# Turning the second batch's normalised input for a linear-attention and FFN kernel: squares of 32 on VectorE and a pass through memory in place of four TensorE transposes

## What is computed

```python
x = x + layernorm(attn(layernorm(x)))
x = x + layernorm(ffn(layernorm(x)))

def attn(h):                                   # 32 heads of 128, blocks of 32 tokens
    q, k, v = silu(h @ qkv_w.T)                # per head
    # scan over blocks with a decayed state kv
    out = (q k^T * diag_decay) v + (q * q_decay) kv
    kv  = kv * block_decay + (k * k_decay)^T v
    return (sigmoid(h @ gate_w.T) * norm_w * rmsnorm(out)) @ out_w.T
def ffn(h):                                    # ternary weights with scales, 512 -> 1792 -> 512
    return (silu(h @ gate.T) * (h @ up.T)) @ down.T
```

## Time and profile before

| what | value |
|---|---|
| median of 3 runs | 2406.01 us (2404.29 to 2406.74) |
| the profiled execution's own time | 2405.24 us |
| its span in the profile | 2403.2 us |
| PE busy | 2355.4 us, 98% of the span, 12276 matmuls |
| DVE busy | 1383.0 us, 58% |
| ACT busy | 1208.9 us, 50% |
| POOL busy | 1679.1 us, 70% |
| DMA | 307.15 MB, mean 128 GB/s |
| granted TensorE clock | 0.995 of full speed over the span |

### The profile page before, as it was taken

How to read it: one execution, slowest core, us unless ns; L and a number is a source line. 1 busy time by engine, 2 the same in 40 slices (tenths; PEclk the granted TensorE clock), 3 DMA queues, 4 the chain that set the end, 5 groups by cost and what they waited for, 6 DMA issues and landing times.

```text
span 2403.2 us, 38344 instructions
## 1 busy us (share of the span) xinstructions
PE 2355.4 (98%) x12276; PEld 2005.5 (83%) x12276; DVE 1383.0 (58%) x2475; ACT 1208.9 (50%) x1748; POOL 1679.1 (70%) x1322
## 2 busy tenths in 40 slices
PE   7999999999999999989999999999999999899997
PEld 6788888888888888878888888888888888788886
DVE  5555555555666666646555555555555555555655
ACT  5555555554444444435454555544444444366563
POOL 4777777777777777756777777777777776474675
PEclk9999999999999999999999999999999999999999
DMA  4344443444444444454444334443333334512212
GB/s 136 127 131 138 137 131 123 134 142 142 145 142 133 129 134 142 156 195 145 141 140 131 126 127 131 131 140 127 119 118 109 109 109 141 181 56 77 79 62 97
DMA packets 165953, 307.15 MB, mean 128 GB/s; under 512 B 22384, under 2 KB 102256, under 8 KB 163184
## 3 DMA queue, kind: packets, MB, share of 16 engines
q1 hardware_dynamic: 138992, 269.93, 34.5%
q10 hardware_dynamic: 26880, 36.18, 4.6%
HBM read 219.02 MB, written 87.03 MB: 127 GB/s over the span
## 4 chain that ended last, share of the span: by engine, by line
PE 86%; ACT 3%; DMA 3%; issue 3%; DVE 3%; POOL 1%; SPq 0%; DVEq 0%; ACTq 0%; POOLq 0%
PE proj L1994 53%; PE yp L1994 18%; PE sc L2041 4%; PE sc L2064 4%; PE sc L2067 4%; PE sc L2054 3%; DMA k_blocks<-pd 1%; DVE pd L1498 1%; ACT piece L1006 0%; ACT k L915 0%; DMA v_tok<-v_blocks 0%; ACT L915 0%; DMA v_blocks<-vf 0%; DMA fs_stage<-ffn_scales 0%; ACT sq L929 0%
## 5 line engine op out<-in xcount | busy, mean ns | idle before, releaser
L1994 PE MATMUL proj<-xb,w_odd 128*128 128x512 f32 x2694 | 705.1, 399 | 5.3 <-ACT g L899 1.8
L1994 PE MATMUL proj<-xb,w_even 128*128 128x512 f32 x2694 | 680.5, 396 | 11.9 <-DMA xb<-x_blocks 3.9
L1994 PEld LDWEIGHTS proj<-xb,w_even 128*128 128x128 f32 x2694 | 498.6, 189 | 114.1 <-issue 7.9
L1994 PEld LDWEIGHTS proj<-xb,w_odd 128*128 128x128 f32 x2694 | 489.5, 189 | 104.6 <-DVE q L1469 5.4
L599 POOL TENSOR_TENSOR qd<-q,table 128x512 f32<-128x512 f32 x128 | 164.0, 1294 | 194.2 <-ACT q L915 194.2
L1543 DVE TENSOR_TENSOR g<-sc,g 128x512 f32<-128x512 f32 x128 | 88.5, 691 | 298.2 <-ACT sq L929 298.2
L590 POOL TENSOR_TENSOR ow_lo<-v_tok,ow_hi 128x1024 fp32r<-128x1024 f32 x32 | 76.7, 2396 | 232.1 <-ACT ow_hi L883 232.1
L1550 DVE TENSOR_TENSOR y<-yp,y 128x512 f32<-128x512 f32 x240 | 164.5, 685 | 120.2 <-PE yp L1994 119.3
L1994 PE MATMUL proj<-x_t,f_hi 128*128 128x512 f32 x896 | 214.2, 392 | 2.7 <-issue 2.7
L1994 PE MATMUL yp<-ow_hi,g_hi 128*128 128x512 f32 x512 | 202.4, 395 | 1.3 <-DVE y L1550 1.3
L1994 PEld LDWEIGHTS proj<-x_t,f_hi 128*128 128x128 f32 x896 | 169.1, 189 | 38.2 <-issue 2.9
(11 more groups left out here) (193 smaller groups left out, 4413.2 us busy)
## 6 DMA issues: line engine op xcount, KB each, us to landing
raw<-w_attn SPq DMA_DIRECT2D x128, 512.0 KB, 3.6
k_blocks<-pd SPq DMA_DIRECT2D x64, 512.0 KB, 3.5
k_tok<-k_blocks SPq DMA_DIRECT2D x256, 128.0 KB, 2.8
v_blocks<-vf SPq DMA_DIRECT2D x64, 512.0 KB, 2.7
v_tok<-v_blocks SPq DMA_DIRECT2D x256, 128.0 KB, 2.8
v_tok<-w_out SPq DMA_DIRECT2D x32, 512.0 KB, 4.5
fraw<-w_ints SPq DMA_DIRECT2D x13, 1024.0 KB, 4.9
piece<-w_ints ACTq DMA_DIRECT2D x21, 512.0 KB, 4.3
```

What stands on the lines that cost most here:

```text
L1994: last = pe.matmul(psum, s, m, start=start and n == 0, stop=n == len(terms) - 1, skip_group_check=more)
```

## The change

TensorE's `turn_piece` and ACT's copy out of PSUM are gone. In their place:

1. DVE (`turn_piece(j, i)`, new) turns the same data in squares of 32 within `piece`, with two instructions of 128 x 256 elements, once ACT has normalised both tiles. It stands behind `keep_s2(w, QQ)` and ahead of `gate(a, 0, 1)`.
2. ACT (`piece_there`, new) issues one DMA of 256 KB that writes them to `p_blocks` in device memory, where `keep_piece` stood.
3. ACT (`piece_back_in`, new) waits for that DMA and issues four DMAs of 64 KB that read them back, so that the squares land in their places on the partitions; it stands behind `activate(w, QQ, OUT22)` and ahead of the two `k_decay(w, 1, ...)`.
4. ACT's `keep_piece` waits for these four and copies from `piece` itself, now behind the two `k_decay(w, 1, ...)`.
5. `mix_piece` moves on DVE from behind `finish_21(w, QQ)` to behind `add_out(a, 2)`, and `piece_high` on ACT from ahead of `activate(w, VV, OUT11)` to behind it.
6. TensorE no longer waits for `piece_normed` and `piece_kept`. Its windows w = 2 to 14 are one loop instead of three; DVE's windows w = 2 to 7 are two loops instead of one.

```diff
--- before.py
+++ after.py
@@ -180,6 +180,7 @@
         piece_in = [sem("piece_in0"), sem("piece_in1")]
         piece_step, piece_sd_ready = sem("piece_step"), sem("piece_sd_ready")
         piece_normed, piece_turned, piece_kept = sem("piece_normed"), sem("piece_turned"), sem("piece_kept")
+        piece_out, piece_back = sem("piece_out"), sem("piece_back")
         piece_mixed, piece_hi_done, piece_lo_done = sem("piece_mixed"), sem("piece_hi_done"), sem("piece_lo_done")
         piece_hi_out, piece_lo_out = sem("piece_hi_out"), sem("piece_lo_out")
         xb_in = [sem(f"xb_in{b}") for b in range(NB)]
@@ -273,6 +274,10 @@
         piece_hi = piece[:, 0:NB * P].bitcast(F32R)
         piece_lo = piece[:, NB * P:2 * NB * P]
         mix = piece_lo.rearrange("p (b n) -> p b n", b=NB)
+
+
+        piece_quads = piece[:, 2 * HID:3 * HID].rearrange("p (b m s t) -> p b m s t", b=QUADS, m=2, s=HALVES)
+        piece_t = piece[:, 0:HID]
         kt = pd[:, 0].rearrange("p h c n -> p (h c n)").rearrange("p (b h c d) -> p b h c d",
                                                                 b=QUADS, h=2, c=CH)
         ow = v_tok[:, :, :, :, :].rearrange("p i h c d -> p (i h c d)").rearrange("p (h n) -> p h n", h=2)
@@ -314,6 +319,7 @@
 
         k_blocks = nc.dram_tensor("k_blocks", (HALVES, QUADS, QUAD, QUADS, 2 * CH * QUAD), F32).ap()
         v_blocks = nc.dram_tensor("v_blocks", (HALVES, QUADS, QUAD, QUADS, 2 * CH * QUAD), F32).ap()
+        p_blocks = nc.dram_tensor("p_blocks", (QUADS, QUAD, QUADS, HID // QUADS), F32).ap()
         x_blocks = nc.dram_tensor("x_blocks", (NB, P, 2, RT, SEG), F32).ap()
         attn_first = nc.dram_tensor("attn_first", (BT, P, HID), F32).ap()
         mid_first = nc.dram_tensor("mid_first", (BT, P, HID), F32).ap()
@@ -1008,12 +1014,25 @@
 
             def keep_piece(j):
 
-                act.wait_ge(piece_turned, j + 1)
-                wait(act, piece_lo_out, 16 * j)
+                act.wait_ge(piece_back, 16 * QUADS * (j + 1))
                 for m in range(2):
-                    act.activation(mix[:, B_21 * m:B_21 * m + T_3 + 1:T_3],
-                                   yp[0][:, 2 * P * m:2 * P * (m + 1)].rearrange("p (s n) -> p s n", s=HALVES),
+                    act.activation(mix[:, B_21 * m:B_21 * m + T_3 + 1:T_3]
+                                   .rearrange("p s (i t) -> p s i t", i=QUADS),
+                                   piece_t.rearrange("p (i m s t) -> p m s i t", i=QUADS, m=2, s=HALVES)[:, m],
                                    ACT.Copy).then_inc(piece_kept, 1)
+
+            def piece_there(j):
+
+                act.wait_ge(piece_turned, 2 * (j + 1))
+                act.dma_start(p_blocks.rearrange("i d b n -> (i d) (b n)"),
+                              piece[:, 2 * HID:3 * HID]).then_inc(piece_out, 16)
+
+            def piece_back_in(j):
+
+                act.wait_ge(piece_out, 16 * (j + 1))
+                for b in range(QUADS):
+                    act.dma_start(piece_t[quad(b)].rearrange("d (i n) -> d i n", i=QUADS),
+                                  p_blocks[:, :, b].rearrange("i d n -> d i n")).then_inc(piece_back, 16)
 
             def piece_high(j):
 
@@ -1074,7 +1093,7 @@
                 square(a, 0, 1)
                 gated_hi(a, 0, 1)
                 if part is not None:
-                    keep_piece(part)
+                    piece_there(part)
                 if checks is not None:
                     look_at_ints(checks + 1)
                 if first_done:
@@ -1086,8 +1105,12 @@
                 activate(w, QQ, OUT22)
                 if finish is not None:
                     store_tile(finish)
+                if part is not None:
+                    piece_back_in(part)
                 k_decay(w, 1, 0)
                 k_decay(w, 1, 1)
+                if part is not None:
+                    keep_piece(part)
                 split_hi_s(w, GG)
                 activate(w, QQ, OUT12)
                 split_hi_a(w, GG)
@@ -1096,9 +1119,9 @@
                 k_decay(w, 0, 0)
                 k_decay(w, 0, 1)
                 square(a, 1, 1)
+                activate(w, VV, OUT11)
                 if part is not None:
                     piece_high(part)
-                activate(w, VV, OUT11)
                 gated_hi(a, 1, 0)
                 gated_hi(a, 1, 1)
                 if part is not None:
@@ -1623,6 +1646,14 @@
                 dve.scalar_tensor_tensor(tile_shift[:, :], tile_meanvar[:, :, 0], -1.0, tile_rstd[:, :],
                                          ALU.mult, ALU.mult).then_inc(piece_step, 1)
 
+            def turn_piece(j, i):
+
+                dve.wait_ge(piece_normed, 2 * (j + 1))
+                for m in range(2):
+                    dve.transpose(piece_quads[:, :, m],
+                                  tiles[:, :, chunk(2 * m + i)].rearrange("p s (b t) -> p b s t", b=QUADS))\
+                        .then_inc(piece_turned, 1)
+
             def mix_piece(j):
 
                 dve.wait_ge(piece_kept, 2 * (j + 1))
@@ -1634,7 +1665,7 @@
                 dve.tensor_tensor(mix[:, T_4], mix[:, B_21], mix[:, T_2], ALU.subtract).then_inc(piece_mixed, 1)
 
             def window(w, first=False, checks=None, rms_of=None, ends_first=False, finish=None, begin=None,
-                       part=None, next_part=False):
+                       part=None, part_half=0, next_part=False):
                 a = w - 1
                 if rms_of is not None:
                     rms(rms_of, yp[0])
@@ -1657,6 +1688,8 @@
                 gate(a, 0, 0)
                 finish_21(w, KK)
                 keep_s2(w, QQ)
+                if part is not None:
+                    turn_piece(part, part_half)
                 gate(a, 0, 1)
                 if finish is not None:
                     tile_lo(finish)
@@ -1675,12 +1708,12 @@
                     dve.wait_ge(attn_out[0], 16)
                 add_out(a, 0, first)
                 finish_21(w, QQ)
-                if part is not None:
-                    mix_piece(part)
                 gate(a, 1, 0)
                 add_out(a, 1, first)
                 keep_s2(w, VV)
                 add_out(a, 2, first)
+                if part is not None:
+                    mix_piece(part)
                 if checks is not None:
                     look_at_block(checks + 1, 1)
                 gate(a, 1, 1)
@@ -1770,9 +1803,11 @@
 
             first_window()
             window(1, first=True, part=0, next_part=True)
-            with dve.Fori(2, 2 * CH) as w:
+            with dve.Fori(2, CH + 1) as w:
                 window(w, part=w - 1, next_part=True)
-            window(2 * CH, part=2 * CH - 1)
+            with dve.Fori(CH + 1, 2 * CH) as w:
+                window(w, part=w - 1, part_half=1, next_part=True)
+            window(2 * CH, part=2 * CH - 1, part_half=1)
             with dve.Fori(2 * CH + 1, PAIRS - 1) as w:
                 window(w, checks=CHECKS_PER_WINDOW * (w - 2 * CH - 1))
             window(PAIRS - 1, checks=WIDTH_CHECKS - CHECKS_PER_WINDOW)
@@ -2068,13 +2103,11 @@
                                          qd[:, s, h, chunk(c)], start=False, stop=True)
                 last.then_inc(attn_done, 1)
 
-            def project_out(a, t, tile=None, downs=0, part=None):
+            def project_out(a, t, tile=None, downs=0):
                 if t == 0:
                     pe.wait_ge(owlo_done, a + 1)
                     if tile is not None:
                         pe.wait_ge(tile_lo_done, tile + 1)
-                    if part is not None:
-                        pe.wait_ge(piece_kept, 2 * (a + 1))
                 if t % CH == 0:
                     pe.wait_ge(glo_done, att_until(a, t // CH, 1))
                 wait(pe, yacc_done, BT * a + t - 1)
@@ -2162,17 +2195,7 @@
                     last = pe.transpose(yp[0][:, chunk(h)], tile_b[:, chunk(h)], ident[:, :])
                 last.then_inc(tile_turned, 1)
 
-            def turn_piece(a, i, j):
-
-                pe.wait_ge(piece_normed, 2 * (j + 1))
-                wait(pe, yacc_done, BT * a - 1)
-                for m in range(2):
-                    for s in range(HALVES):
-                        last = pe.transpose(yp[0][:, chunk(2 * m + s)], tiles[:, s, chunk(2 * m + i)],
-                                            ident[:, :])
-                last.then_inc(piece_turned, 1)
-
-            def window(w, x_wait=False, rms_of=None, tile=None, part=None):
+            def window(w, x_wait=False, rms_of=None, tile=None):
                 a = w - 1
                 if rms_of is not None:
                     sums_of_squares(rms_of, yp[0])
@@ -2191,8 +2214,6 @@
                     turn_tile(a, tile)
                 product(w, QQ, 6)
                 attend(a, 0, 1)
-                if part is not None:
-                    turn_piece(a, part, a)
                 product(w, QQ, 7)
                 product(w, QQ, 2)
                 contributions(a, 1, 0)
@@ -2202,7 +2223,7 @@
```

(10 more changed lines are left out.)

## The result

The change makes the kernel slower: 2443.24 us (2440.19 to 2444.13, 4 runs) against 2405.15 us of the kernel before in the same session; the ratio is 1.015, 95% interval 1.0138 to 1.0162. The forecast was 2412, range 2404 to 2421: the sign was right, the size was not. The span of the profiled execution is 2438.3 us, 35.1 more than before.

A forecast was written before the change was run, and what follows sets the result against it. PE was taken to set the time, with the ACT-DVE chain and the write to `k_blocks` delaying QQ 3 and QQ 4. 2405.24 + 4.0 (write) + 2.1 (way back) = 2411.3, with 0.77 to the median 2412 us; range 2404 to 2421.

The forecast's parts named there:

- the sentence on `mix_piece`: On DVE: the moved four instructions, about 1 us, fit a gap before the last `gate`, whose reader waits for PE: 0.
- The write to `p_blocks`: ACT's write delays SP's write to `k_blocks`, and with it QQ 4: 0.5 us a window, +4.0 us.
- The bound of 0.7: Upper bound per window for that delay, from window 9: a write out after 4.09 us instead of 3.38 beside a 512 KB load.
- wholly in front: Compared with window 9's load, the new write starts earlier and lies entirely ahead of the write to `k_blocks`; 0.5 us taken.
- The way back: ACT's wait for the four reads, plus its copy, delays the values towards KK 5 of the next window: 0.3 each, +2.1 us.
- The lag itself: ACT from the split on: 0.5 us idle plus 0.64 copy, 1.6 us later, 1.1 later against PE.
- The rival with the chance of 0.2: Reads land late behind key traffic, ACT's lag passes 1.6 us, each window repeats window 6: 2419 to 2424; chance 0.2.
- The removed transposes: Four a window on PE, at most 0.9 us with idle; PE waits 0.9 us longer at QQ 3 instead: worth 0.
- DVE's new transposes: Two on DVE, 0.7 us together, fit its 1.76 us of idle before the `gate`: 0.
- if it were shorter: The ACT-DVE chain covers the removed transposes; were it shorter by 0.9 us, all of that would be gained.
- the rivals on the slow side: Slower than the forecast: late reads behind key traffic, 2419 to 2424, chance 0.2.
- The signs of being wrong: Windows of 63.5 us, QQ 3 as in window 10, `k_blocks` out as before, DVE's transposes over 1.7 us, or KK 5 idle each window.

The follow-up runs named there:

- Extra_quarter: The kernel before the change plus an unread 64 KB write from ACT's queue ahead of SP's write to `k_blocks`: 2407.02 us, ratio 1.0004.
- extra_load: The kernel before the change plus a 256 KB load from memory on ACT's queue ahead of SP's write to `k_blocks`: 2415.05 us, ratio 1.0044.
- mix_back: The changed kernel with DVE's `mix_piece` put back behind `finish_21(w, QQ)`: 2429.21 us.
- keep_back: The changed kernel without its five DMAs, with `mix_piece` and ACT's `keep_piece` both in their old places: 2408.40 us.

## Why the prediction was wrong

**The step that failed** is the sentence on `mix_piece`, "(four short instructions, about 1 us) moves into a gap before the last `gate`", whose price is 0. No row stands beside it. A gap is there, in window 4 of the kernel before 1.29 us:

```profile
305.30 0.69 DVE L1543 TENSOR_TENSOR g<-sc,g 128x512 f32<-128x512 f32 x1 [1.29 <-ACT sq L929]
```

The 1.15 us that the four take while POOL is idle would have fitted. In the new place POOL is in its splits and each of the four waits for it: 5.1 us. "Waits for PE anyway" named the reader of the gate only; behind the four on DVE stand `add_out` and the finish that VV 3 waits for as well. Undone in the change it gives 14.0 us, added alone it costs 9.1: a quarter to over a third of the 38.

**The write to `p_blocks`** was right in mechanism and place, and mis-sized: 8.8 us added alone (8.5 undone in the change) instead of 4.0. The bound of 0.7 came from window 9, where the other transfer started after the write to `k_blocks`. Here it stands ahead. Extra_quarter and extra_load show that bytes count, so "half the bytes" was a fair argument; what is left to explain the size is "wholly in front", which no run varied by itself.

**The way back** was right in mechanism and mis-sized: taken at 2.1 us, with 1.25 a window as the other end. The reads' traffic costs 3.6, and 8.4 remain for the wait with the copy. The lag itself was about right in window 4 of the change: ACT idles 0.49 us for the piece and copies for 0.72, where 0.5 and 0.64 were said, and `w_odd` is 1.4 us later against QQ 4 instead of 1.1. What it costs further on was not: in mix_back KK 5 waits in six windows. The rival with the chance of 0.2 describes it, but its price is too small as well: by its own terms 8 x 0.7 + 7 x 1.25 is 14.4 us, so 2420 and not the 2424 stated, and the five DMAs cost 20.8 us in mix_back. In the change itself KK 5 doesn't wait, since the stall at VV 3 comes first.

**Right steps.** The removed transposes gave nothing back: QQ 3 stands at 22.63 us in both kernels, and PE waits 0.80 us where 0.9 was said. DVE's new transposes fit at their place (0.76 us for the two instead of 0.7, with 1.09 us of idle left). The chain of ACT and DVE is what makes a window with a piece long: shortened, it gave 8.6 us. That the transposes would be gained "if it were shorter" holds in some windows and not in the total.

**How it adds up.** From 2405.2: what is left without memory and with `mix_piece` back, +3.2; the traffic, +12.4; the wait for the piece, +8.4; `mix_piece`, +14.0; together 2443.2. It closes by construction, since the 8.4 are what the others leave, and the 12.4 were measured on the kernel before and carried over. Two of the parts were also measured the other way round: 14.0 and 9.1, 8.8 and 8.5. The first don't agree. The four subtractions take equally long in both kernels, but in the change they start 3 us later in the window and VV 3 waits longer for them. The trade between VV 3 and KK 5 works the other way and makes the 14.0 smaller. So the parts depend on each other, and none of them is a price that holds elsewhere. The 3.2 us of the first rung are not explained: not by the copy's place (keep_back), and 1 us of them is lost by window 9 and 2.75 in window 16, at the change of batch (76.87 us against 74.12).

The range, which ends at 2421, failed twice over. With `mix_piece` back in its place the kernel takes 2429.2 us, so the two terms of the DMA path alone, 6.1 us where nearly 21 were measured, would have broken it. And the rivals on the slow side were about that path alone; none was about a line that the diff only moves. The signs of being wrong had the same hole: none of them came true, and none looked at `mix_piece`.
